# A fused two-layer block on one core: the first stage in another order, and feature chunks read contiguously

## The chip, the cores and the metric

The kernel runs on one core of one Trainium2 chip. The metric is the device time in microseconds; runs of the kernel before took 401.86, 402.31 and 403.27 us, median 402.31. One program computes everything: PE (matrix products), DVE and ACT (vector and scalar work), POOL, and SP, which issues the transfers, each follow a list of instructions of their own and wait for each other through counting semaphores.

## The reference

Six blocks are added one after the other to x, which is 2 sequences of 64 tokens with 512 features, so 128 rows:

```python
x = x + _L0_xattn_ref(_layernorm(x), ctx_512, Wq, w_kc_q, w_kc_kv, W_qr, W_kr, Wo)
x = x + _L0_attn_ref(_layernorm(x), wq, wk, wv, wo)        # weights replaced by sign(w) * mean|w|
x = x + _L0_ffn_ref(_layernorm(x), gate_w, w_gate, w_up, w_down)   # 32 experts, top 8
x = x + _L1_xattn_ref(_layernorm(x), ctx_512, Wq, Wkv_expand, Wout)
x = x + _L1_attn_ref(_layernorm(x), w_qkv, w_g, w_proj, gn_weight, gn_bias)
x = x + _L1_ffn_ref(_layernorm(x), w_router, w_gate, w_up, w_down, ...)
```

Most of the change is in the first block, an attention over a context of 1024 tokens with 16 heads:

```python
q_big = einsum('bshk,hkq->bshq', (hidden_q @ Wq.T).reshape(b, s, H, K), w_kc_q)
kv_rope = kv_c * cos + rotate_half(kv_c) * sin
q_r = einsum('bshq,hqr->bhsr', q_big, W_qr)
k_r = einsum('bld,hdr->bhlr', kv_rope, W_kr)
attn = softmax(einsum('bhsr,bhlr->bhsl', q_r, k_r))
ctx_c = einsum('bhsl,bld->bhsd', attn, kv_rope)
out = einsum('bhsd,hkd->bshk', ctx_c, w_kc_kv).reshape(b, s, H * K) @ Wo.T
```

## The kernel before

All data are 32-bit floats. The weights of the first block come in four groups of four heads. For each group g, PE does five things, and the program names them so:

- `queries(g)` (L988): the query projection, 16 products of 128 columns, from `in_wq` (1024 KB) and the transposed x, `xnT`.
- `qrk_products(g)` (L978): w_kc_q times W_qr of the four heads, from `in_wr` (1152 KB, the rank weights), 12 products whose outputs are 64 partitions high: even heads go to PSUM partitions 0 to 63, odd heads to 64 to 127 (column halves).
- `qkw_products(g)` (L1012): that times W_kr (`in_wkr`, 512 KB), 4 products over 64 rows. These are the key products.
- `latent_queries(g)` (L1022): that times the queries, 4 products. Its result, `qk_x`, is the query in the space of the context.
- `context_transposes(g)` (L1001): a quarter of the rotated context, 4 transposes.

An instruction of this kind on 32-bit data appears twice in the trace (16 products are x32). Between them DVE copies from PSUM: `at_copy` (L631) after qrk, `bw_copy` (L637) after qkw, `qk_copy` (L643) after latent; ACT copies the queries (L426) and the context (L422). The rotation of the context is shared by POOL (L385, the swapped half times sine, into `rope_tmp`) and DVE (L621, times cosine; L624, the addition). SP issues all transfers on one queue in a fixed order. `keep_clock(n)` (L957) is n products that nobody reads, which keep PE busy while it has nothing to do.

Then come 16 units of one head pair and one sequence (the unit loop): two products of scores (L1056), DVE's row maximum (L666), ACT's exponential (L439), eight transposes (L1066), copied half by ACT (L447) and half by DVE (L673), eight context products (L1075), a reciprocal (L677) and a scaling on DVE (L681), one transpose (L1084) and its copy (L452). They are pipelined: in step i PE does the scores of unit i, the transpose of result i-3, the context products of unit i-2 and the transposes of unit i-1. The next block's weights (`we`, from `in_e`) lie in SBUF by then; for them DVE sums absolute values (L696, in steps 8 to 11: 2048, 512, 512 and 2048 columns), and ACT takes all signs at once (L472, 5120 columns, in step 12).

Wherever x is transposed (L965, six times; L1214, twice; L1387, once) and in the gather of rows for the experts (L1263), the 512 features are split into four chunks with feature 4q+c in chunk c, so that a chunk is every fourth number of a row; the weights are laid out to match.

## Time and profile before

| what | value |
|---|---|
| profiled execution | 405.05 us, of which the span is 403.0 us |
| PE | busy 382.4 us, 95% of the span |
| DVE, ACT, POOL | 38%, 21%, 6% of the span |
| transfers | 79.41 MB, 197 GB/s mean; first part of the program about 300 to 450 GB/s |
| DVE in a unit (L666, L673, L677, L681) | 1.22, 0.69, 0.15 and 0.35 us |
| ACT in a unit (L439, its read-out, L447, L452) | 1.12, 0.19, 0.59 and 0.28 us |
| gather (L1263) on the chain of waits | groups of four at 0.91 or 0.92 us (ten) and 1.04 us (two), one of eight at 1.98 us |
| output projection of the retention (L1391) | 8 instructions, 5.41 us from 348.49; granted clock 0.50 from 350 to 352 us |

The span is the time from the first to the last instruction; what lies around it belongs to the execution too. The chain of waits is read backwards by the profiler, from the last instruction to what released it. A row of the timeline gives the start, the duration, the engine, the line, and in brackets how long the engine stood idle before it and who released it. The granted clock is a share of 2.4 GHz.

### The profile page before, as it was taken

How to read it: one execution, taken by the hardware profiler on the slowest of the kernel's cores; microseconds unless marked ns; L12 is line 12 of the kernel's file. 1: busy time of each engine (PE TensorE's matmuls, PEld its weight loads, DVE VectorE, ACT ScalarE, POOL GpSimd, SP SyncE). 2: the span in 40 equal slices, each digit the busy share in tenths (PEclk: the TensorE clock that was granted, in tenths of full speed). 3: DMA queues.
4: the chain of work that ended last, by engine and by line, in shares of the span. 5: the costliest groups of instructions: out<-in, count | busy, mean ns of one | idle time of the engine just before them, and what ended most of it. 6: DMA issues, size and time to landing. Idle time of an engine off the chain costs nothing.

```text
span 403.0 us, 5245 instructions
## 1 busy us (share of the span) xinstructions
PE 382.4 (95%) x2175; PEld 240.8 (60%) x2175; DVE 151.3 (38%) x326; ACT 85.0 (21%) x163; POOL 23.5 (6%) x45
## 2 busy tenths in 40 slices
PE   9898899999889999999999999999989999899997
PEld 7787668777678575666444544444356546564456
DVE  3164254576632145235022222222265344544221
ACT  1001144434742004102121212212102024101011
POOL 1050000000000010011000000000020100000220
PEclk9899999999999999999999999999999999899999
DMA  8999699800003200060798889989689600000000
GB/s 306 362 422 445 228 426 433 344 2 0 2 0 110 126 2 0 2 260 2 262 386 313 340 337 325 371 298 443 260 337 423 285 0 2 0 2 0 0 0 26
DMA packets 7591, 79.41 MB, mean 197 GB/s; under 512 B 977, under 2 KB 1745, under 8 KB 2513
## 3 DMA queue, kind: packets, MB, share of 16 engines
q1 hardware_dynamic: 7568, 79.09, 49.8%
q8 instruction: 17, 0.28, 0.3%
q14 instruction: 6, 0.04, 0.0%
HBM read 78.82 MB, written 0.26 MB: 196 GB/s over the span
## 4 chain that ended last, share of the span: by engine, by line
PE 80%; DVE 10%; issue 3%; DMA 3%; POOL 2%; ACT 1%; SPq 0%; ACTq 0%; DVEq 0%; POOLq 0%
PE ps L1276 9%; PE ps L1404 9%; PE ps L1075 6%; PE ps L1056 4%; PE ps L1303 4%; PE ps L1301 4%; PE ps L1348 3%; PE ps L1114 3%; PE ps L1263 3%; PE ps L988 3%; PE ps L1308 3%; PE ps L1066 3%; PE ps L1236 3%; DMA rd<-in_wkr 3%; PE ps L1219 2%
## 5 line engine op out<-in xcount | busy, mean ns | idle before, releaser
L957 PE MATMUL ps<-ones 128*128 128x256 bf16 x305 | 38.7, 279 | 1.0 <-POOL ones L368 1.0
L1276 PE MATMUL ps<-rd,ra 128*64 128x384 f32 x224 | 39.2, 492 | 0.0
L957 PEld LDWEIGHTS ps<-ones 128*128 128x128 bf16 x305 | 30.1, 100 | 8.3 <-issue 3.2
L1075 PE MATMUL ps<-rd,ra 128*128 128x128 f32 x256 | 31.4, 276 | 0.0
L1075 PEld LDWEIGHTS ps<-rd,ra 128*128 128x128 f32 x256 | 29.9, 192 | 2.3 <-issue 2.0
L1056 PE MATMUL ps<-rd 128*128 128x512 f32 x64 | 30.0, 594 | 0.7 <-DVE rd L643 0.7
L1276 PEld LDWEIGHTS ps<-rd,ra 128*64 128x64 f32 x224 | 14.8, 136 | 25.6 <-issue 25.6
L1404 PE MATMUL ps<-rd,xnT 128*128 128x512 f32 x64 | 28.0, 594 | 0.0
L439 ACT ACTIVATE ra<-ps,sv 128x1024 f32<-128x1024 f32 x16 | 17.8, 1115 | 37.9 <-DVE sv L666 37.9
L831 DVE COPY xnT<-ps 128x512 f32<-128x512 f32 x14 | 9.7, 691 | 39.5 <-PE ps L1303 39.5
L666 DVE TENSOR_REDUCE sv<-ps 128x1 f32<-128x1024 f32 x16 | 19.6, 1223 | 8.5 <-PE ps L1056 8.5
L673 DVE COPY ra<-ps 128x512 f32<-128x512 f32 x16 | 11.1, 692 | 25.1 <-PE ps L1066 25.0
L1404 PEld LDWEIGHTS ps<-rd,xnT 128*128 128x128 f32 x64 | 11.9, 190 | 14.2 <-issue 14.2
L817 DVE SCALAR_TENSOR_TENSOR ra<-ra,ps 128x192 f32<-128x192 f32 x14 | 5.0, 354 | 40.9 <-ACT ra L516 40.9
L516 ACT ACTIVATE ra<-ps 128x192 f32<-128x192 f32 x14 | 4.6, 331 | 61.0 <-PE ps L1276 61.0
L1066 PE MATMUL ps<-cst,ra 128*128 128x128 f32 x128 | 16.6, 273 | 0.8 <-ACT ra L439 0.8
L1263 PEld LDWEIGHTS ps<-ra,xn 128*128 128x128 f32 x56 | 14.8, 321 | 3.6 <-issue 2.4
L988 PE MATMUL ps<-xnT,ra 128*128 128x128 f32 x128 | 16.9, 295 | 0.0
L988 PEld LDWEIGHTS ps<-xnT,ra 128*128 128x128 f32 x128 | 16.2, 209 | 0.4
L1056 PEld LDWEIGHTS ps<-rd 128*128 128x128 f32 x64 | 11.0, 190 | 9.1 <-issue 8.1
L1308 PE MATMUL ps<-xnT,ra 128*128 128x512 f32 x28 | 14.5, 601 | 1.4 <-DVE xnT L831 1.4
L1303 PE MATMUL ps<-rd,ra 128*128 128x512 f32 x28 | 15.8, 645 | 0.0
(231 smaller groups left out, 501.9 us busy)
## 6 DMA issues: line engine op xcount, KB each, us to landing
rd<-in_ring SPq DMA_DIRECT2D x16, 2304.0 KB, 9.0
rd<-in_f1gu SPq DMA_DIRECT2D x8, 1024.0 KB, 13.2
rb<-in_wb SPq DMA_DIRECT2D x1, 5120.0 KB, 35.5
ra<-in_e SPq DMA_DIRECT2D x2, 2560.0 KB, 9.4
rb<-in_b SPq DMA_DIRECT2D x1, 5120.0 KB, 20.2
ra<-in_wr SPq DMA_DIRECT2D x4, 1152.0 KB, 16.5
ra<-in_wq SPq DMA_DIRECT2D x4, 1024.0 KB, 20.4
ra<-in_f1s SPq DMA_DIRECT2D x1, 2048.0 KB, 29.3
```

Source lines behind the costliest of these rows:

```text
L439: act.activation(prob_x[u % 2].rearrange("p j l -> p (j l)"), ps[:, 2 * (u % 2):2 * (u % 2) + 2, :].rearrange("p a n -> p (a n)"), ACT.Exp ...
L666: dve.tensor_reduce(mx_x[:, u:u + 1], ps[:, 2 * (u % 2):2 * (u % 2) + 2, :].rearrange("p a n -> p (a n)"), AX.X, ALU.max, negate=True).the ...
L957: pe.matmul(ps[:, bank, 0:256], idle[:, 0:P], idle, start=True, stop=True)
L988: ins = pe.matmul(ps[:, g % 2, h * P:(h + 1) * P], wq_x(g)[:, c, h * P:(h + 1) * P], xnT[:, c, :], start=(c == 0), stop=(c == C - 1))
L1056: ins = pe.matmul(ps[:, 2 * (u % 2) + half, :], rows, kvT[:, u % 2, half * 512:half * 512 + 512], start=True, stop=True)
L1066: ins = pe.transpose(ps[:, 4 + half, j * P:(j + 1) * P], prob_x[u % 2][:, 4 * half + j, :], ident)
L1075: ins = pe.matmul(ps[:, 6, 0:P], probT_x[u % 2][:, j, :], kvr[:, u % 2, j, :], start=(j == 0), stop=(j == J - 1))
L1263: ins = pe.matmul(ps[:, half, c * 256:(c + 1) * 256], src[:, 2 * half + c, :], placed[:, 4 * q:4 * q + 4, :].rearrange("p e s -> p (e s)") ...
L1276: ins = pe.matmul(ps[CAP * e:CAP * e + CAP, 2 + p % 2, 0:2 * I0].rearrange("p (g n) -> p g n", g=2), moe_xq[q % 2][:, c, CAP * e4:CAP * e4 ...
L1303: pe.matmul(ps[:, 4, :], hT[:, 1, :], slot_down[j][:, 2, :], start=False, stop=True).then_inc(dn_done, 1)
L1308: return pe.matmul(ps[:, 7, :], moe_hT_even[(p - DENSE) // 2 % 2][:, 2 + p % 2, :], moe_y, start=False, stop=last)
L1404: ins = pe.matmul(ps[:, bank, 0:n], xnT[:, c, :], w[:, c, lo:lo + n], start=(c == 0), stop=(c == C - 1))
```

## The change

The transfers of the first stage begin with x, the constants, the query weights and then the rank weights of each group. `in_wkr` is laid out on 128 partitions with half the columns, even heads on 0 to 63 and odd heads on 64 to 127. PE's list begins with the transposes of x and the queries, and the last key product and the last latent product stand between the first scores.

On PE, from the start of the program to the second pair of scores, the instructions of before are these (the first line is `keep_clock`):

```order
L957 MATMUL ps<-ones 128x256 x44
L978 MATMUL ps<-ra 64x128 x12
L965 MATMUL ps<-cst,xn 128x128 x4
L957 MATMUL ps<-ones 128x256 x16
L1012 MATMUL ps<-rd 128x128 x4
L988 MATMUL ps<-xnT,ra 128x128 x16
L978 MATMUL ps<-ra 64x128 x12
L1022 MATMUL ps<-rd 128x128 x4
L1012 MATMUL ps<-rd 128x128 x4
L988 MATMUL ps<-xnT,ra 128x128 x16
L978 MATMUL ps<-ra 64x128 x12
L1022 MATMUL ps<-rd 128x128 x4
```

and now, where L962 are the transposes of x, L987 the queries, L975 qrk, L1013 the key products and L1023 latent:

```order
L954 MATMUL ps<-ones 128x256 x40
L962 MATMUL ps<-cst,xn 128x128 x4
L954 MATMUL ps<-ones 128x256 x16
L987 MATMUL ps<-xnT,ra 128x128 x16
L975 MATMUL ps<-ra 64x128 x12
L987 MATMUL ps<-xnT,ra 128x128 x16
L1013 MATMUL ps<-rd 128x128 x4
L975 MATMUL ps<-ra 64x128 x12
L1023 MATMUL ps<-rd 128x128 x4
L987 MATMUL ps<-xnT,ra 128x128 x16
L1013 MATMUL ps<-rd 128x128 x4
L1000 MATMUL ps<-cst,rd 128x128 x4
```

The first two groups of queries have moved ahead of the first key products, and the third stands before any context transpose.

On PE at the end of the stage, before (L1047 transposes `ctx64`, L1056 are the scores, L1066 the transposes of the first unit):

```order
L988 MATMUL ps<-xnT,ra 128x128 x16
L1001 MATMUL ps<-cst,rd 128x128 x4
L1022 MATMUL ps<-rd 128x128 x4
L1047 MATMUL ps<-cst,ctx 128x128
L1056 MATMUL ps<-rd 128x512 x4
L1066 MATMUL ps<-cst,ra 128x128 x8
```

and now (L1037 are the scores, L1049 the transposes of the first unit):

```order
L1000 MATMUL ps<-cst,rd 128x128 x4
L1023 MATMUL ps<-rd 128x128 x4
L1037 MATMUL ps<-rd 128x512 x2
L1013 MATMUL ps<-rd 128x128 x4
L1037 MATMUL ps<-rd 128x512 x2
L1023 MATMUL ps<-rd 128x128 x4
L1110 MATMUL ps<-cst,ctx 128x128
L1049 MATMUL ps<-cst,ra 128x128 x8
```

A key product and a latent product now stand between the scores and the transposes that need the first exponential.

On DVE in a unit with a sum of absolute values, before (L666 row maximum, L673 copy, L677 and L681 reciprocal and scaling, L696 the sum):

```order
L666 TENSOR_REDUCE sv<-ps 128x1
L673 COPY ra<-ps 128x512
L677 RECIPROCAL sv<-sv 128x1
L681 TENSOR_SCALAR xn<-ps,sv 128x128
L696 TENSOR_REDUCE sv<-ra 128x1
```

and now (L659, L670, L674, L666, L693 in the same sense):

```order
L659 TENSOR_REDUCE sv<-ps 128x1
L670 RECIPROCAL sv<-sv 128x1
L674 TENSOR_SCALAR xn<-ps,sv 128x128
L666 COPY ra<-ps 128x512
L693 TENSOR_REDUCE att_st<-ra 128x1
```

The scaling has moved ahead of the copy; the sum is one of six, of at most 1024 columns.

The diff, cut to its core:

```diff
-        rope_tmp = rd[:, 4096:5120].rearrange("p (j d) -> p j d", j=J)
+        rope_tmp = [rd[:, 3072 + 1024 * b:4096 + 1024 * b].rearrange("p (j d) -> p j d", j=J) for b in range(B)]
+        we_parts = [(0, 0, 1024), (1, 2048, 2560), (2, 2560, 3072), (3, 3072, 4096), (0, 1024, 2048), (3, 4096, 5120)]
...
             sp.dma_start(x[:, :], x_in).then_inc(ld_x, 16)
-            rank_weights(0)
             sp.dma_start(cst[:, :], consts_d).then_inc(ld_const, 16)
             query_weights(0)
-            sp.dma_start(rd[0:R0, 11264:13312], wkr_d).then_inc(ld_kr, 16)
+            rank_weights(0)
+            sp.dma_start(rd[:, 11264:12288], wkr_d).then_inc(ld_kr, 16)
+            query_weights(1)
             rank_weights(1)
             sp.dma_start(rd[:, 0:2048], ctx_d).then_inc(ld_ctx, 16)
             sp.dma_start(rd[:, 2048:3072], rope_d).then_inc(ld_ctx, 16)
-            for g in range(1, GROUPS):
-                if g > 1:
-                    rank_weights(g)
+            for g in range(2, GROUPS):
                 query_weights(g)
+                rank_weights(g)
...
+            sp.wait_ge(q_ps, 3)
+            sp.wait_ge(at_ps, 3)
+            sp.dma_start(we, e0_d).then_inc(ld_e0, 16)
             sp.wait_ge(qk_ps, GROUPS)
-            sp.dma_start(we, e0_d).then_inc(ld_e0, 16)
...
-                if i == 12:
-                    act.wait_ge(asum_done, 4)
-                    act.activation(we, we, ACT.Sign).then_inc(sign_done, 1)
+                if 6 <= i < 12:
+                    _, a0, a1 = we_parts[i - 6]
+                    act.wait_ge(asum_done, i - 5)
+                    act.activation(we[:, a0:a1], we[:, a0:a1], ACT.Sign).then_inc(sign_done, 1)
...
-                src = xn[:, :].rearrange("p (q c) -> p c q", c=C)
+                src = xn[:, :].rearrange("p (c q) -> p c q", c=C)
...
-                for h in range(4):
-                    ins = pe.matmul(ps[:, 4 + g % 2, h * P:(h + 1) * P], qrk[0:R0, 4 * g + h, :], wkrT[0:R0, 4 * g + h, :],
-                                    start=True, stop=True)
+                for j in range(2):
+                    for odd in range(2):
+                        rows = slice(odd * R0, odd * R0 + R0)
+                        ins = pe.matmul(ps[:, 4 + odd, j * P:(j + 1) * P], qrk[rows, 2 * g + j, :], wkrT[rows, 2 * g + j, :],
+                                        start=True, stop=True)
...
             def scores(u):
-                if u == 0:
-                    pe.wait_ge(qk_sb, GROUPS)
+                pe.wait_ge(qk_sb, u // 4 + 1)
+                if u < 2:
+                    pe.wait_ge(kvT_sb, 2 * u + 2)
+                    pe.wait_ge(q_sb, GROUPS)
+                    pe.wait_ge(at_sb, GROUPS)
```

POOL no longer waits for DVE between the two halves of the rotation, DVE copies qrk in one piece instead of two, and `bw_copy` reads both PSUM banks of the row halves at once; each key product now waits for the copy of the one before. The same contiguous split stands in the transposes of L1214, L1387 and L1448 and in the gather, and every weight that meets such a chunk is laid out by rows of 128 on the host, with rows as long as before.

## Rows read from the trace of the kernel before

**Rows 1.** Chain of waits, 0 to 54 us: start us, us, what

```profile
2.57 10.43 DMA rd<-in_wkr
...
14.26 5.39 PE ps L988 x32
19.66 1.46 PE ps L978 x24
21.12 1.09 PE ps L1022 x8
...
26.49 3.20 POOL rd L385 x2
...
29.78 1.23 DVE rd L624
...
32.99 3.77 PE ps L988 x32
```

**Rows 2.** Timeline of PE, 0 to 54 us: start us, us, then idle before

```profile
0.98 6.42 PE L957 MATMUL ps<-ones 128*128 128x256 bf16 x44 [0.98 <-POOL ones L368]
...
9.38 1.91 PE L957 MATMUL ps<-ones 128*128 128x256 bf16 x16
13.14 1.13 PE L1012 MATMUL ps<-rd 64*128 64x128 f32 x8 [1.85 <-DMA rd<-in_wkr]
...
31.83 1.16 PE L1012 MATMUL ps<-rd 64*128 64x128 f32 x8 [1.79 <-DVE rd L631]
...
45.72 1.13 PE L1022 MATMUL ps<-rd 128*128 128x128 f32 x8 [0.30 <-issue]
...
47.70 3.70 PE L1056 MATMUL ps<-rd 128*128 128x512 f32 x8 [0.74 <-DVE rd L643]
52.23 1.09 PE L1066 MATMUL ps<-cst,ra 128*128 128x128 f32 x8 [0.84 <-ACT ra L439]
```

**Rows 3.** Windows: busy us, then PEclk, DMA share, GB/s

```profile
14.00:16.00 2.00, 2.00 (x11) 1.88 (x10) 0.69 (x1) 0.00 (x0) 0.00 (x0) 0.55 1.02 424
...
8.00:14.00 6.00, 4.15 (x44) 3.56 (x40) 1.53 (x3) 0.00 (x0) 0.00 (x0) 1.00 1.01 295
14.00:34.00 20.00, 18.21 (x160) 16.91 (x159) 9.89 (x15) 1.79 (x3) 5.46 (x4) 0.91 1.05 434
```

**Rows 4.** Chain of waits, 60 to 128 us: the scores of three units

```profile
75.65 1.72 PE ps L1056 x4
...
80.14 1.72 PE ps L1056 x4
...
114.37 1.72 PE ps L1056 x4
```

**Rows 5.** Timeline of SP's queue: issue of the third rank weights

```profile
5.26 0.45 SPq L289 DMA_DIRECT2D ra<-in_wr  x1
```

**Rows 6.** DMA issues of the window 5.2 to 5.5 us: us to landing last

```profile
DMA to landing us min/median/max: 20.5/20.5/20.5
```

**Rows 7.** Timeline, 80 to 121 us, of DVE, ACT and PE

```profile
85.73 2.28 DVE L696 TENSOR_REDUCE sv<-ra 128x1 f32<-128x2048 f32 x1
...
104.97 4.48 ACT L472 ACTIVATE ra<-ra 128x5120 f32<-128x5120 f32 x1
...
120.09 0.33 PE L1084 MATMUL ps<-cst,xn 128*128 128x128 f32 x1 [1.24 <-DVE xn L681]
```

**Rows 8.** Weight loads by form, 200 to 210 us: busy us, mean ns

```profile
L1263 PEld LDWEIGHTS ps<-ra,xn 128*128 128x128 f32 x7 | 1.9, 321 | 0.4 <-issue 0.2
...
L1308 PEld LDWEIGHTS ps<-xnT,ra 128*128 128x128 f32 x2 | 0.3, 191 | 0.0
```

**Rows 9.** Chain of waits, 145 us to the end

```profile
145.99 0.76 PE ps L965 x4
...
308.00 0.66 PE ps L1191 x4
...
394.99 1.73 PE ps L1425 x8
```

More of the change, by code:

```diff
@@ L623, in rope @@
                 dve.wait_ge(rope_swap, b + 1)
-                dve.tensor_tensor(kvr[:, b], kvr[:, b], rope_tmp, ALU.add).then_inc(rope_ready, 1)
+                dve.tensor_tensor(kvr[:, b], kvr[:, b], rope_tmp[b], ALU.add).then_inc(rope_ready, 1)
             def at_copy(g):
                 dve.wait_ge(at_ps, g + 1)
-                heads = qrk[0:R0, 4 * g:4 * g + 4, :].rearrange("p (j two) k -> p two j k", two=2)
-                for odd in range(2):
-                    ins = dve.tensor_copy(heads[:, odd], ps[odd * R0:odd * R0 + R0, 2 + g % 2, 0:2 * P].rearrange(
-                        "p (j k) -> p j k", j=2))
-                ins.then_inc(at_sb, 1)
+                dve.tensor_copy(qrk[:, 2 * g:2 * g + 2, :].rearrange("p j k -> p (j k)"),
+                                ps[:, 2 + g % 2, 0:2 * P]).then_inc(at_sb, 1)
             def bw_copy(g):
                 dve.wait_ge(bw_ps, g + 1)
-                dve.tensor_copy(qkw[:, 4 * g:4 * g + 4, :].rearrange("p h t -> p (h t)"), ps[:, 4 + g % 2, :]).then_inc(bw_sb, 1)
+                dve.tensor_copy(qkw[:, 4 * g:4 * g + 4, :].rearrange("p (j two) d -> p two j d", two=2),
+                                ps[:, 4:6, 0:2 * P].rearrange("p two (j d) -> p two j d", j=2)).then_inc(bw_sb, 1)
             def qk_copy(g):
@@ L654, in _ @@
             rope(1)
-            for g in range(2, GROUPS):
-                at_copy(g)
-                qk_copy(g - 1)
-                bw_copy(g)
-            qk_copy(GROUPS - 1)
-            dve.wait_ge(c64T_ps, 1)
-            dve.tensor_copy(ctx64T[:, :], ps[:, 7, 0:P]).then_inc(c64T_ready, 1)
+            bw_copy(1)
+            at_copy(2)
+            qk_copy(1)
+            bw_copy(2)
+            at_copy(3)
+            qk_copy(2)
             def row_max(u):
@@ L983, in queries @@
                 pe.wait_ge(ld_q[g], 16)
+                if g == 0:
+                    pe.wait_ge(xT_ready, 1)
                 if g >= 2:
@@ L1092, in latent_values @@
                 ins.then_inc(lat_ps, 1)
+            pe.wait_ge(consts_ready, 1)
+            keep_clock(40)
+            pe.wait_ge(ld_const, 16)
+            x_transposes(0)
+            queries(0)
+            qrk_products(0)
+            queries(1)
+            qkw_products(0)
+            qrk_products(1)
+            latent_queries(0)
+            queries(2)
+            qkw_products(1)
+            context_transposes(0)
+            qrk_products(2)
+            context_transposes(1)
+            latent_queries(1)
+            queries(3)
+            context_transposes(2)
+            qkw_products(2)
+            qrk_products(3)
+            context_transposes(3)
+            latent_queries(2)
             for i in range(UNITS + 3):
@@ L1096, in _ @@
                     scores(i)
+                if i == 0:
+                    qkw_products(GROUPS - 1)
+                if i == 1:
+                    latent_queries(GROUPS - 1)
+                    pe.wait_ge(kvT_sb, GROUPS)
+                    pe.wait_ge(ld_c64, 16)
+                    pe.transpose(ps[:, 7, 0:P], ctx64[:, :], ident).then_inc(c64T_ps, 1)
                 if i == UNITS + 1:
@@ L1119, in _ @@
             latent_values(3)
-            pe.wait_ge(asum_done, 4)
+            pe.wait_ge(asum_done, 6)
             pe.wait_ge(consts_ready, 2)
-            pe.matmul(ps[:, 5, 0:4], ones[:, :], asum, start=True, stop=True).then_inc(wsum_ps, 1)
+            for half in range(2):
+                ins = pe.matmul(ps[:, 5, 0:4], ones[:, :], asum[:, half], start=(half == 0), stop=(half == 1))
+            ins.then_inc(wsum_ps, 1)
             output_product(range(8, 12))
@@ L1510 @@
     cst, rope, xpos, decay = constants()
-    wq = v["L0_xattn_Wq"].T.reshape(P, C, GROUPS, 512)
+    rows = lambda w: w.reshape(-1, P, w.shape[1]).transpose(1, 0, 2).reshape(P, -1)
+    wq = rows(v["L0_xattn_Wq"].T).reshape(P, C, GROUPS, 512)
     wkcq = v["L0_xattn_w_kc_q"].transpose(2, 0, 1).reshape(P, KQ, H0, P)
@@ L1522 @@
     q0 = v["L0_attn_wq"].T.reshape(D, 8, 4, 16).transpose(0, 2, 1, 3).reshape(D, D)
[L1523 to L1525 removed]
+    e0 = np.concatenate([rows(q0), rows(v["L0_attn_wk"].T), rows(v["L0_attn_wv"].T), rows(v["L0_attn_wo"].T)], axis=1)
+    pair = lambda w: w.reshape(PAIRS, 2, C, P, I0).transpose(0, 3, 1, 2, 4).reshape(PAIRS, P, -1)
     wd = v["L0_ffn_w_down"].reshape(PAIRS, 2, I0, D)
```

111 lines of the change are left out of this document (44 added, 67 removed).

## The prediction

> **What bounds the kernel now.** I read the busy time first: PE is busy for 95% of the span (the table), so only work taken off PE, PE's own gaps and PE's clock can be worth anything. DVE and ACT count only where PE stands behind them. Then I read the chain of waits of the first 54 us. After one transfer (wkr, 10.43 us from issue to landing) it is PE nearly throughout, but for one stretch in which POOL and DVE rotate the context [rows 1]. PE's timeline shows its gaps there: 1.85 us for wkr, 1.79 us for a DVE copy queued behind the rotation, then 0.30, 0.74 and 0.84 us where the first score unit waits for the last copies and the first exponential [rows 2]. That is 5.5 us. After the first gap the granted clock is 0.55 of full from 14 to 16 us, so mostly the lower level, 1.2 GHz [rows 3], and the 32 query products of the first group take 5.39 us on the chain, against 3.77 us for a later group at full clock [rows 1]. In the unit loop the scores stand 4.49 us apart while nothing disturbs them (75.65 and 80.14), and PE has no gap: PE bounds it. But from 80.14 to 114.37 seven units take 34.23 us, not 31.43: 2.8 us lost [rows 4].
>
> **First stage.** By its new order PE runs 40 idle products, the transposes, queries(0), qrk(0), queries(1), qkw(0), qrk(1), latent(0), queries(2), and so on. Only one product sits where the new wait falls, so I walk there. The idle products take 6.42/44 = 0.146 us each from 0.98 us on [rows 2], so 40 end at 6.8 us, 0.6 us before the 7.4 of now. x and the constants are the first two transfers, and queries(0)'s weights make 1510 KB in all. Now x, the first rank weights and the constants are 1638 KB and have landed when the transposes run, ahead of the 16 idle products of 9.38 [rows 2]; so queries(0) has its data when the new 16 (1.91 us) end, at 6.8 + 0.6 + 1.9 = 9.3 us. Then, at full-clock durations, query 3.77, qrk 1.46, query 3.77, qkw 0.85 (below), qrk 1.46, latent 1.09 [rows 1]: PE stands before queries(2) at 21.7 us.
>
> When do its weights land? Before them lie 256+230+1024+1152+512+1024+1152+1024+512 KB, with them 7910 KB. Now the rank weights of group 2 complete 8038 KB and land at 5.26+20.5 = 25.8 us [rows 5, 6]; at 434 GB/s 128 KB less are there 0.3 us sooner, at 25.5 us. But wkr now fills 128 partitions instead of 64. From 8 to 14 us, when it goes through, the queues move 295 GB/s at a DMA share of 1.01, against 434 GB/s from 14 to 34 us at 1.05 [rows 3]. At 434 the 1.77 MB of those 6 us would take 4.1 us: 1.9 us earlier. So 23.6 us, and PE waits 1.9 us (bounds: 0 if copies delay PE by as much, 3.8 if the port gain fails). Beside it, the Trainium skill, page "SBUF — State Buffer", section "Door 1: The DMA port swizzle", says that partitions 0 to 63 reach 8 of 16 ports. By its about 218 GB/s against 436 for 512 KB this would be an estimate of 1.2 us; the trace's drop is wider, and I keep its 1.9.
>
> A wait of 1.85 us was followed by the low clock, one of 1.79 us (from 30.04) was not. A wait of 1.9 us before queries(2) is nearest to the first, so I count the fall once more: 5.39-3.77 = 1.6 us lost.
>
> The rotation: POOL's two buffers let it run both batches without waiting for DVE. Now its second swap takes 3.20 us in the chain, then 1.23 us of DVE [rows 1], then copies, then PE. With context and tables landed at about 21 us, two swaps of at most 3.2 us and a 1.23 us addition end by 28.7 us. PE needs the first batch after queries(2) and qkw(1), at 23.6+5.4+0.85 = 29.9 us. So the rotation hides, with 1 us to spare; the copy queued behind it (0.69 us) is wanted by latent(1), another 2.4 us on. The last key product and latent(3) move beside the first scores, so that 1.16+1.13 us of PE work stands where PE waited 0.74 and 0.84 us [rows 2]; DVE takes their copies after the first row maxima, while scores(1) (1.7 us) runs. I take all these gaps (5.5 us) as gone, cost zero.
>
> Key products in row halves: four pieces of 1.16 us [rows 2], each 4 products on 64 rows. The trace has no row pair. Its nearest row is column halves (L978): 24 instructions in 1.46 us against 8 in 1.09 us for whole ones (L1022) [rows 1], 0.061 against 0.136 us each, so halves do run together. But those loads are 64 columns wide and these are 128, and a load is nearly as long as its product. Bounds: no gain, or 0.55 of the time, 0.5 us saved a piece; a loss of 0.1 us a piece if switching costs what one issue gap does. I take the middle, 0.25 us, 1.0 us in all, since the slow load is the nearer likeness.
>
> The Trainium skill, page "TensorEngine Tiling (Array Packing)", section "Key Properties", says that changing the tiling mode drains TensorE. By that the pieces would gain less. The rows show qrk (column halves) from 19.66 for 1.46 us and whole products from 21.12 [rows 1], without a pause between them; for row halves no row here shows it, and a drain of 0.1 us at each of eight changes would make the time 0.8 us longer.
>
> Sum of the stage: 5.5 + 1.6 + 0.6 + 1.0 - 1.9 - 1.6 = 5.2 us gained at the third pair of scores (now 53.32).
>
> **Sums and signs in pieces.** DVE's reduction over 2048 columns takes 2.28 us and delays the next row maximum; ACT's sign over 5120 takes 4.48 us and the exponential behind it starts late; PE then waits [rows 7]. The pieces are at most 1024 wide: by the same rates 1.2 and 0.9 us. In a free unit DVE works 1.22+0.69+0.15+0.35 = 2.4 us and ACT 1.12+0.19+0.59+0.28 = 2.2 us of 4.49 (the table), and a piece fits in what is left. So the 2.8 us go. e0 is issued earlier, behind wb; it lands well before the sixth unit. Also the scaling of the context now stands ahead of the copy of the transposed probabilities. At the loop's end PE waits 1.24 us for that scaling (L681), which DVE does after copy and reciprocal [rows 7]. In the new order it is done during the transposes, and the context product then waits only for the copy (0.69 us): 0.5 us. Loop: 3.3 us. One more tiny product for the sums: nothing I can tell.
>
> **Contiguous chunks.** The gather's weight loads read every fourth number: 321 ns, against 191 ns for L1308's contiguous ones [rows 8]. Four gather products take 0.91 to 1.04 us on the chain (the table), where 8 of the same width with contiguous loads take 1.73 us [rows 9], 0.87 us for four. Over 56 of them (one group of 8 at 1.98, two of 4 at 1.04, ten at 0.91) it is 13.2 against 12.1 us: 1.1 us. The transposes of xn take 0.76 us for four, those of contiguous data 0.66 us [rows 9]; nine such groups stand alone on the chain: 0.9 us. Together 2.0 us (bounds 0 and 2.3).
>
> The same page on SBUF, section "Door 1", says that fp32 may stride by 4 for free. By that this part would bring nothing. The loads' 321 against 191 ns [rows 8] speak against it, so it is a rival with a small chance.
>
> **Sum.** 5.2 + 3.3 + 2.0 = 10.5 us. The profiled execution took 405.05 us for its span of 403.0; it would take 394.6. It lies 2.7 us over the median of the runs, 402.31, and I take the same difference off that: 391.8 us.
>
> **Rivals.**
> - The clock holds after the wait for queries(2), as after 1.79 us now: 391.8 - 1.6 = 390.2 us. For it: the two gaps differ by 0.06 us only. Chance 0.24.
> - The row halves run fully together (1.0 us more) and the clock holds: 389.2 us. For it: column halves do. Against: width of the loads. Chance 0.10. With these goes the stretch at 348 us, where the clock is at 0.50 after two short gaps and eight projection products cost 5.41 us for some 3.4 (the table). It may fall otherwise when all lies 10 us earlier: 2.0 us to the good.
> - The transfers land as late as now: queries(2) waits 3.8 us: 393.7 us. Against: 295 GB/s only while wkr passes. Chance 0.13.
> - Strided loads are hidden behind their products: no 2.0 us: 393.8 us. Chance 0.06.
> - The pieces still hold up the loop, since sums and signs now touch six units: the 2.8 us stay, 394.6 us. Against: DVE's 2.4 us of 4.49. Chance 0.05.
> - Slower than before: PE waits for each of the query weights in turn and the clock stays at its low level from the first query product on. Low clock costs (5.39-3.77)/3.77 = 0.43 of the work; the stage has 33 us of it: 14.2 us more, less the 1.6 counted: 391.8 + 12.6 = 404.4 us. It decides from about 28 us of full-clock work done at the low level ((10.5 + 1.6)/0.43). Against: now the next group at 19.66 runs at its full-clock 1.46 us [rows 1] once work flows, and I see only one wait. Chance 0.02.
> The forecast itself has 0.40.
>
> **Numbers.** Forecast 391.8 us. Range 388.4 to 394.6 us: it holds the forecast, the clock, port and load cases, and leaves out some 0.1 at each side. A difference of 0.3% (1.2 us) is what a measurement of this kernel can tell from none. Faster by more: 0.96; within: 0.02; slower: 0.02.
>
> **What would show it.** In the changed profile: PE without a gap until about 21.7 us, then one gap of about 2 us before queries(2) on in_wq, and the clock low in the next stretch; no gap at the context transposes; key products of 0.9 us a group; third scores near 48 us; scores 4.49 us apart to the end of the loop; the gather's loads near 190 ns and 0.87 us for four. I am wrong if a wait for a copy replaces the gaps, if the 0.5 clock spreads over several query products, or if loads stay at 320 ns.

## The result, and the profile after

The changed kernel takes 391.86 us (median of 4 runs, 390.99 to 393.28); on the same chip the kernel before took 402.79 us (4 runs). The ratio is 0.9713, with a 95% interval of 0.9668 to 0.9758. The forecast of 391.8 us was met. Its terms were not all right, though: three of them were off by 0.8 to 1.8 us each, and the errors cancelled by luck.

Line numbers have shifted: queries L987, qrk L975, key products L1013, latent L1023, context transposes L1000, scores L1037, transposes of the first unit L1049, residual projection L1128, gather L1279, output projection of the retention L1407, `keep_clock` L954.

PE's timeline after, start of the program to the scores, answers to [rows 2]:

```profile
0.98 5.90 PE L954 MATMUL ps<-ones 128*128 128x256 bf16 x40 [0.98 <-POOL ones L371]
...
9.55 3.84 PE L987 MATMUL ps<-xnT,ra 128*128 128x128 f32 x32 [0.48 <-DMA ra<-in_wq]
13.32 1.53 PE L975 MATMUL ps<-ra 128*64 128x128 f32 x24
16.05 3.84 PE L987 MATMUL ps<-xnT,ra 128*128 128x128 f32 x32 [1.21 <-DMA ra<-in_wq]
19.82 0.71 PE L1013 MATMUL ps<-rd 64*128 64x128 f32 x8
20.46 1.53 PE L975 MATMUL ps<-ra 128*64 128x128 f32 x24
21.93 1.16 PE L1023 MATMUL ps<-rd 128*128 128x128 f32 x8
25.08 3.84 PE L987 MATMUL ps<-xnT,ra 128*128 128x128 f32 x32 [1.99 <-DMA ra<-in_wq]
28.84 0.71 PE L1013 MATMUL ps<-rd 64*128 64x128 f32 x8
29.49 0.66 PE L1000 MATMUL ps<-cst,rd 128*128 128x128 f32 x4
```

The old gaps (for wkr, for the copy behind the rotation, and the three small ones at the first scores) are gone. In their place PE waits three times, 3.68 us in all, and each time for query weights. After its first product, which waits 0.98 us for POOL as before, it waits nowhere in the first 47 us for DVE, ACT or POOL.

The windows of [rows 3] after (busy us of PE, PEld, DVE, ACT, POOL, then PEclk, DMA share, GB/s):

```profile
8.00:14.00 6.00, 5.52 (x54) 5.04 (x54) 0.52 (x3) 0.58 (x1) 0.00 (x0) 1.00 1.01 421
14.00:16.00 2.00, 0.85 (x16) 0.60 (x12) 0.42 (x1) 0.02 (x1) 0.00 (x0) 1.00 1.02 420
14.00:34.00 20.00, 16.80 (x177) 15.25 (x174) 11.43 (x13) 2.41 (x5) 6.46 (x4) 1.00 1.05 437
```

The transfers run at 421 GB/s where they ran at 295, and the granted clock is 1.00 in all three windows, although PE stood still for 1.99 us. So every query group takes 3.74 or 3.84 us, the first too. Before, it took 5.39 us on the chain [rows 1], and in the same view as above:

```profile
14.19 5.46 PE L988 MATMUL ps<-xnT,ra 128*128 128x128 f32 x32
```

The chain of waits after, at the scores and in the first part of the loop:

```profile
42.56 0.65 PE ps L1013 x8
...
46.99 1.72 PE ps L1037 x4
...
100.74 1.72 PE ps L1037 x4
105.23 1.73 PE ps L1037 x4
```

The third scores start at 46.99 instead of 53.32 us: the stage is 6.3 us shorter. From there to the last scores at 105.23 us thirteen units take 58.24 us, 4.48 each, without the 2.8 us that were lost in [rows 4]; the first product of the residual projection starts at 117.97 in the timeline of PE, where it was 127.61. Of this 9.6 us the stage holds 6.3 and the loop 3.3.

The end of the loop on PE, and DVE in a unit with a sum, which answer to [rows 7]:

```profile
110.25 0.30 PE L1069 MATMUL ps<-cst,xn 128*128 128x128 f32 x1 [0.53 <-ACT ra L451]
```

```profile
82.82 0.69 DVE L666 COPY ra<-ps 128x512 f32<-128x512 f32 x1 [0.47 <-PE ps L1049]
83.43 1.21 DVE L693 TENSOR_REDUCE att_st<-ra 128x1 f32<-128x1024 f32 x1
84.56 1.21 DVE L659 TENSOR_REDUCE sv<-ps 128x1 f32<-128x1024 f32 x1
```

The wait of 1.24 us for the scaling has become 0.53 us for a copy of ACT, and the row maximum follows at once on the sum.

Behind the loop, in the chain of waits, the first gather group and the projection of the retention:

```profile
178.32 1.73 PE ps L1279 x8
...
337.32 3.71 PE ps L1407 x8
```

and the weight loads of the gather, 195 to 205 us (busy us, mean ns), which answer to [rows 8]:

```profile
L1279 PEld LDWEIGHTS ps<-ra,xn 128*128 128x128 f32 x4 | 0.8, 190 | 0.5 <-issue 0.5
```

The loads take 190 ns where they took 321. The group of eight went from 1.98 to 1.73 us, the groups of four to 0.86 or 0.87, and four transposes from 0.76 to 0.67. Over 13 gather groups and the eight groups of transposes behind the loop that is 1.8 to 1.9 us. Another 1.7 us comes from L1407, 3.71 against 5.41 us, and the change has no part in that: before, the granted clock was 0.50 from 350 to 352 us, and after it is 1.00 there. PE's waits just ahead of these products are the same in both (0.79 and 0.78 us before, 0.79 twice after).

The profiled execution took 391.82 us, 13.2 us less than that of before, but the medians are only 10.9 us apart. The profile of before had its clock at the lower level in two places, which cost 3.3 us in all (1.6 and 1.7), and an execution of before does not always have them (below).

### The profile page after: what moved, and what is told of

It reads as the page before. It is cut to its first block, busy times and chain, and to the rows that moved or that the text cites. A ratio compares the mean times of both kernels' runs of the same rounds, so it can differ in the third digit from the quotient of the medians.

```text
span 390.0 us, 5266 instructions
## 1 busy us (share of the span) xinstructions
PE 374.0 (96%) x2173; PEld 231.6 (59%) x2173; DVE 151.9 (39%) x324; ACT 85.4 (22%) x168; POOL 24.6 (6%) x46
## 4 chain that ended last, share of the span: by engine, by line
PE 83%; DVE 8%; DMA 5%; SPq 1%; POOL 1%; issue 1%; ACT 0%; POOLq 0%; DVEq 0%
PE ps L1292 10%; PE ps L1420 9%; PE ps L1037 7%; PE ps L1060 7%; DMA ra<-in_wq 5%; PE ps L1319 4%; PE ps L1317 4%; PE ps L1364 4%; PE ps L1128 4%; PE ps L1049 3%; PE ps L1324 3%; PE ps L1279 3%; PE ps L1252 3%; PE ps L1235 2%; PE ps L1173 2%; PE ps L987 2%
## 5 line engine op out<-in xcount | busy, mean ns | idle before, releaser
L954 PE MATMUL ps<-ones 128*128 128x256 bf16 x301 | 38.2, 279 | 1.0 <-POOL ones L371 1.0
L954 PEld LDWEIGHTS ps<-ones 128*128 128x128 bf16 x301 | 29.6, 100 | 8.1 <-issue 3.2
L1037 PE MATMUL ps<-rd 128*128 128x512 f32 x64 | 30.2, 594 | 0.0
L659 DVE TENSOR_REDUCE sv<-ps 128x1 f32<-128x1024 f32 x16 | 19.6, 1223 | 10.7 <-PE ps L1037 10.7
L987 PE MATMUL ps<-xnT,ra 128*128 128x128 f32 x128 | 15.3, 277 | 3.7 <-DMA ra<-in_wq 3.7
L987 PEld LDWEIGHTS ps<-xnT,ra 128*128 128x128 f32 x128 | 14.6, 192 | 4.4 <-DMA ra<-in_wq 4.4
L1049 PE MATMUL ps<-cst,ra 128*128 128x128 f32 x128 | 16.6, 273 | 0.0
L1037 PEld LDWEIGHTS ps<-rd 128*128 128x128 f32 x64 | 10.9, 190 | 7.8 <-issue 7.6
L1317 PE MATMUL ps<-rd,ra 128*64 128x512 f32 x56 | 15.1, 618 | 0.0
L1364 PE MATMUL ps<-rb,xnT 128*128 128x512 f32 x32 | 14.3, 595 | 0.2 <-DVE xnT L599 0.2
## 6 DMA issues: line engine op xcount, KB each, us to landing
rd<-in_f1gu SPq DMA_DIRECT2D x8, 1024.0 KB, 13.2
ra<-in_f1s SPq DMA_DIRECT2D x1, 2048.0 KB, 25.8
```

The source lines that it names most:

```text
L659: dve.tensor_reduce(mx_x[:, u:u + 1], ps[:, 2 * (u % 2):2 * (u % 2) + 2, :].rearrange("p a n -> p (a n)"), AX.X, ALU.max, negate=True).the ...
L954: pe.matmul(ps[:, bank, 0:256], idle[:, 0:P], idle, start=True, stop=True)
L987: ins = pe.matmul(ps[:, g % 2, h * P:(h + 1) * P], wq_x(g)[:, c, h * P:(h + 1) * P], xnT[:, c, :], start=(c == 0), stop=(c == C - 1))
L1037: ins = pe.matmul(ps[:, 2 * (u % 2) + half, :], rows, kvT[:, u % 2, half * 512:half * 512 + 512], start=True, stop=True)
L1049: ins = pe.transpose(ps[:, 4 + half, j * P:(j + 1) * P], prob_x[u % 2][:, 4 * half + j, :], ident)
L1317: pe.matmul(ps[CAP * e:CAP * e + CAP, 4, :], hT[:, 0, CAP * e:CAP * e + CAP], slot_down[j][:, e, :], start=True, stop=False)
```

## Experiments

**1. Only the contiguous chunks (c_only).** The kernel before with the new layout of the features, the weights laid out to match, and nothing else:

```diff
-                src = xn[:, :].rearrange("p (q c) -> p c q", c=C)
+                src = xn[:, :].rearrange("p (c q) -> p c q", c=C)
...
```

> The kernel before with the contiguous feature chunks alone. My theory: gather products from 13.2 to about 12.1 us on the chain of waits and nine groups of four transposes from 0.76 to 0.67 us, 1.9 us in all, so about 400.6 us where the kernel before takes 402.5. Rival (the loads are hidden behind their products): within 0.5 us of the kernel before. What the profile shows at the projection after 346 us (5.41 us before, 3.71 us after the change) should not depend on this edit but on the clock: 5.4 or 3.7 us, with a granted clock that goes with it.

Measured: 401.12 us (nine runs from 399.75 to 402.93 and one of 405.86) against 402.47, ratio 0.9964, interval 0.9938 to 0.9989. In its chain of waits:

```profile
186.48 1.73 PE ps L1263 x8
194.00 0.87 PE ps L1263 x4
...
345.47 3.71 PE ps L1391 x8
```

The gather and the transposes have the durations of the changed kernel, so the part stands alone and is worth 1.8 us in the trace; the medians show 1.4 us, within the interval. L1391 takes 3.71 us here too, in the old order of the first stage: its 5.41 us belonged to one execution and not to the kernel.

**2. Only the loop (l_only).** The kernel before with the sums and signs in six pieces and the scaling ahead of the copy:

```diff
-                if 1 <= i <= UNITS:
-                    probT_copy(i - 1)
                 if i >= 2:
                     ctx_scale(i - 2)
+                if 1 <= i <= UNITS:
+                    probT_copy(i - 1)
...
+                if 9 <= i < 15:
+                    _, a0, a1 = we_parts[i - 9]
+                    act.wait_ge(asum_done, i - 8)
+                    act.activation(we[:, a0:a1], we[:, a0:a1], ACT.Sign).then_inc(sign_done, 1)
...
```

> The kernel before with the sums and signs in six pieces of at most 1024 columns (in the units 8 to 13 for the sums, 9 to 14 for the signs) and the scaling ahead of the copy. My theory: scores stand 4.49 us apart from 53 us to the end of the loop, and the loop is 3.3 us shorter: about 399.2 us against 402.5. Rival (the pieces only spread the stall over more units): units of more than 4.6 us, and less than 1 us gained.

Measured: 399.5 us (398.15 to 401.73, 8 runs), ratio 0.9927, interval 0.9887 to 0.9967: 3.0 us by the medians. Three of its scores in the chain of waits:

```profile
60.50 1.72 PE ps L1056 x4
...
105.39 1.72 PE ps L1056 x4
109.87 1.73 PE ps L1056 x4
```

Eleven units take 49.37 us, 4.49 each. The loop's term holds by itself.

**3. The old order in DVE's unit (old_scale).** The changed kernel with the copy of the transposed probabilities ahead of the scaling again (the first two hunks of the diff above, backwards).

> The changed kernel with DVE's old order in a unit: the copy of the transposed probabilities ahead of the scaling of the context. By my sum the new order is worth 0.5 us, all at the end of the loop: PE waits about 1.2 us for the scaling there again, in place of a shorter wait for the copy, and the time is near 392.3 us. Rival, the new order is worth nothing there because the copy is as late: the same stretch from the last scores to the context product keeps its length, and the time stays at 391.9 us.

Measured: 393.36 us (392.91 to 393.82, 4 runs), ratio 0.9753, interval 0.9688 to 0.9818. In its timeline the old wait of [rows 7] is back, to the hundredth:

```profile
111.60 0.33 PE L1069 MATMUL ps<-cst,xn 128*128 128x128 f32 x1 [1.24 <-DVE xn L674]
```

From the third scores (47.64 us on its chain) to the first product of L1128 (119.12) it takes 71.48 us, against 70.98 in the changed kernel: the 0.5 us predicted. The medians differ by 1.5 us. Of the rest, 0.65 us is the later start of the third scores in its profile; three of its four executions have a mean clock of 0.996, which is not this order's doing either. The first stage is that of the changed kernel, and here PE waits much longer before queries(2), without a fall of the clock behind it:

```profile
25.63 3.84 PE L987 MATMUL ps<-xnT,ra 128*128 128x128 f32 x32 [3.15 <-DMA ra<-in_wq]
```

**4. Halves in turn, or one kind after the other (same_half).** A first theory was that the key products gain because neighbours in the list lie on different rows. Here the two even ones come first:

```diff
-                for j in range(2):
-                    for odd in range(2):
+                for odd in range(2):
+                    for j in range(2):
```

> The changed kernel with its four key products of a group in another order: both of the upper half, then both of the lower, instead of in turn. Theory (products on different row halves run together): a group of 8 instructions takes about 1.0 us instead of 0.65, because only the middle two differ in their half; the first stage is up to 1.0 us longer (three of the four groups are past the last wait for weights). Rival (the 0.65 us come from something else, as the copy layout or the banks): 0.65 us as now, no difference.

Measured: 391.34 us (390.38 to 391.69, 4 runs), ratio 0.9722, interval 0.9699 to 0.9744.

```profile
19.44 0.72 PE L1013 MATMUL ps<-rd 64*128 64x128 f32 x8
```

The group takes 0.72 us against 0.71 in the changed kernel: this theory falls. The order inside a group of four makes no difference.

**5. All four on the same rows (one_half).** The banks, the order and the layout of the transfer stay those of the changed kernel; only the products of odd heads are computed from the even heads' rows.

```diff
-                        rows = slice(odd * R0, odd * R0 + R0)
+                        rows = slice(0, R0)
```

> The changed kernel with all four key products of a group read from partitions 0 to 63, into the same two PSUM banks and in the same order; so the products of the odd heads are those of the even heads' numbers, and the output is not the reference's. Row halves as the cause: nothing can run side by side any more, and a group of key products takes about 1.1 us in the timeline of PE as before, with its eight weight loads near 0.96 us, instead of 0.71 and 0.52; four groups make it 1.6 to 1.8 us slower than the changed kernel, near 393.4 us. Rival, the two banks or the smaller transfer layout as the cause: a group stays at 0.71 us and the time at 391.9 us.

Measured: 392.81 us (391.88 to 394.3, 4 runs), ratio 0.9728, interval 0.9663 to 0.9793. Its timeline of PE, and its loads from 18 to 22 us:

```profile
21.11 1.16 PE L1013 MATMUL ps<-rd 64*128 64x128 f32 x8
```

```profile
L1013 PEld LDWEIGHTS ps<-rd 64*128 64x128 f32 x8 | 1.0, 187 | 0.1
```

and the same view of the changed kernel:

```profile
L1013 PEld LDWEIGHTS ps<-rd 64*128 64x128 f32 x8 | 0.5, 186 | 0.1
```

The group is back at 1.16 us. The two PSUM banks and the wide transfer bring nothing to it: it is the row halves. One load still lasts 187 ns, but eight are busy for 1.0 us in one case and for 0.5 in the other, so the loads lie over each other more when their halves differ. The time shows less of it than the 1.6 to 1.8 us expected, 1.0 us between the medians: from queries(2) to the third scores it takes 23.1 us on the chain (26.39 to 49.47) against 21.9, which holds three of the four groups, and the first group lies ahead of a wait. Whether two halves could also write into one bank was not tried.

**6. W_kr in two transfers of 64 partitions (kr_two).** Same bytes, same places, but each transfer fills one half of the partitions:

```diff
-            sp.dma_start(rd[:, 11264:12288], wkr_d).then_inc(ld_kr, 16)
+            sp.dma_start(rd[0:R0, 11264:12288], wkr_d[0:R0]).then_inc(ld_kr, 16)
+            sp.dma_start(rd[R0:P, 11264:12288], wkr_d[R0:P]).then_inc(ld_kr, 16)
...
-                    pe.wait_ge(ld_kr, 16)
+                    pe.wait_ge(ld_kr, 2 * 16)
```

> The changed kernel with the 512 KB of W_kr moved as two transfers of 64 partitions each instead of one of 128. Theory (a transfer to 64 partitions moves at about half the rate): 256+256 KB at about 210 GB/s, some 1.2 us later for everything behind; waits for query weights grow by about that, from 1.21 to 2.4 us before queries(1) and with no further growth before queries(2), and the time is 1.2 us longer (393.0), or 2.8 longer if the clock falls after the longer wait. Rival (the transfers overlap, since the two halves use different ports, or the slowness had another reason): 421 GB/s from 8 to 14 us as now, no difference.

Measured: 395.01 us (394.01 to 396.43, 4 runs), ratio 0.9811, interval 0.9786 to 0.9835: 3.2 us of the gain gone, more than either number expected. Timeline of PE, then windows:

```profile
20.20 6.60 PE L988 MATMUL ps<-xnT,ra 128*128 128x128 f32 x32 [4.74 <-DMA ra<-in_wq]
```

```profile
8.00:14.00 6.00, 5.55 (x52) 5.19 (x51) 1.16 (x3) 0.48 (x1) 0.00 (x0) 1.00 1.02 273
...
20.00:26.00 6.00, 5.80 (x27) 5.80 (x28) 0.00 (x0) 0.00 (x0) 0.00 (x0) 0.50 1.02 423
```

The rate from 8 to 14 us falls to 273 GB/s, below the 295 of [rows 3], and the weights of queries(1) land 4.1 us later, at 20.2 us instead of 16.0. PE waits 4.74 us, and the clock goes to 0.50 behind it: that group takes 6.60 us. So the 128 partitions are what made the transfers faster. The one rival left by this run alone, two transfers instead of one, falls with the kernel before, which had a single transfer of 64 partitions: its order of transfers shows 295, 324, 303 and 329 GB/s from 8 to 14 us in four profiles, against 415 to 427 in the nine profiles in which W_kr goes to 128 partitions at once. The Trainium skill, page "SBUF — State Buffer", section "Door 1: The DMA port swizzle", says that 64 partitions reach half of the ports; the direction agrees with this trace. By the section's about 218 GB/s for 64 partitions against 436 for 128, 512 KB would lose 1.2 us, an estimate; the trace shows 4.1 us at the transfer behind (2.9 us against the latest of the other profiles with the changed kernel's order of transfers, 17.3 us in experiment 5): the measurement decides.

**7. The weights of queries(2) ahead of the context (wq2_early).** If the wait of 1.99 us is the loss, it should go when these weights come sooner:

```diff
+            query_weights(2)
             sp.dma_start(rd[:, 0:2048], ctx_d).then_inc(ld_ctx, 16)
             sp.dma_start(rd[:, 2048:3072], rope_d).then_inc(ld_ctx, 16)
-            for g in range(2, GROUPS):
-                query_weights(g)
-                rank_weights(g)
+            rank_weights(2)
+            query_weights(3)
+            rank_weights(3)
```

> The changed kernel with the third query weights ahead of the context and the rope tables. Theory (PE waits 1.99 us because the 1536 KB of context and tables lie ahead): the weights are there 3.7 us sooner and this wait is gone, but the tables land at about 25 us instead of 22.6, POOL and DVE rotate until some 34 us, and PE waits for the first context transposes instead, at about 27 us, for 1 to 3 us: the time changes by -1 to +1 us. Rival (the rotation has slack): 2 us shorter, 389.9 us.

Measured: 395.16 us (394.34 to 395.89, 4 runs), ratio 0.9818, interval 0.979 to 0.9846: 3.3 us slower than the changed kernel, where -1 to +1 us was expected.

```profile
22.80 3.74 PE L988 MATMUL ps<-xnT,ra 128*128 128x128 f32 x32
26.46 0.71 PE L1014 MATMUL ps<-rd 64*128 64x128 f32 x8
30.63 1.09 PE L1001 MATMUL ps<-cst,rd 128*128 128x128 f32 x4 [3.45 <-DVE rd L621]
31.65 2.63 PE L976 MATMUL ps<-ra 128*64 128x128 f32 x24
```

The wait is gone and a longer one stands in its place: the rotation now starts later (POOL at 24.98 us instead of 22.63), and PE stands 3.45 us before the context transposes, after which the clock is low (24 products of qrk in 2.63 us instead of 1.53). The old wait hid the rotation. I had given it 1 us to spare in my prediction; moving one 1 MB transfer was enough to lose that cover.

**8. Idle products in the waits (fill).** Ten before queries(1) and 16 before queries(2):

```diff
+            keep_clock(10)
             queries(1)
...
+            keep_clock(16, 7)
             queries(2)
```

> The changed kernel with 10 idle products in the wait before queries(1) and 16 in the one before queries(2), which fit in the waits. Theory (the clock held in these waits in all runs): no difference, 391.9 us. Rival (the clock falls in some runs, which makes the spread from 390.99 to 393.28 us): the runs lie within 1 us of each other near 391 us.

Measured: 392.53 us (391.98 to 393.05, 4 runs), ratio 0.975, interval 0.9722 to 0.9779. queries(2) starts at 25.26 us, as without them (25.08): the idle products end at 25.19, and on the chain of waits the weights land at 25.21, so the transfer still sets this point. Four executions, one of them at a mean clock of 0.996, don't tell whether the filling keeps the clock up more often.

**9. The kernel before once more (before2).** No edit.

> The kernel before once more, for the granted clock of each of its executions. If the half clock at 14 and at 348 us (1.6 and 1.7 us) belongs to the kernel, every execution shows a mean clock near 0.992 and times near 402.5; if it is chance, executions without one or the other lie 1.6 to 3.3 us lower and show up to 1.000.

Measured: 402.69 us (401.66 to 405.71, 10 runs). In its profiled execution (402.68 us) the low clock stands at another place than in [rows 2]:

```profile
13.99 3.84 PE L988 MATMUL ps<-xnT,ra 128*128 128x128 f32 x32
...
22.77 5.46 PE L988 MATMUL ps<-xnT,ra 128*128 128x128 f32 x32 [1.31 <-DMA ra<-in_wq]
```

The first query group has the full clock here, and one group later it falls, after a wait of 1.31 us. Of 58 timed executions of this kernel on four chips whose mean clock is known, 19 have 0.999 or 1.00 and took 401.5 to 402.5 us, 20 have 0.996 (402.3 to 403.8), 14 have 0.992 (404.0 to 405.7) and 5 have 0.987 (406.2 to 408.9). The profile with one fall has a mean of 0.996 and the one with two 0.992, so each fall seems to take 0.004 off it, and 0.987 would be three, which no profile here shows. A fall is something that an execution has or has not, and the profiled 405.05 us was one with two.

The first waits differ as well. In place of 1.85 us for wkr and 1.79 us behind the rotation [rows 2], this profile has 0.40 us and none, and the 1.31 us before queries(1) instead. Experiments 1 and 2, which keep this first stage, have 0.87 and 1.04 us, then 1.62 and 1.40 us before queries(1), then 0.74 us behind the rotation in both, and their clock held. The last three waits (0.30, 0.74 and 0.84 us) are the same in all four profiles.

**10. The changed kernel once more (after_again).** No edit.

> The changed kernel itself once more, beside the version with the queries first on the same chip. Executions at full clock should lie at 391 to 393 us. If the start of the stage is a matter of how the transfers come in an execution, the wait before queries(2) varies by some tenths of a microsecond to 1.5 us from the 1.99 us of the first profile, and with it the third pair of scores (46.99 us).

Measured: 393.04 us (390.41 to 394.65, 6 runs) against 404.13 (11 runs), ratio 0.9731, interval 0.9686 to 0.9776.

```profile
15.72 3.84 PE L987 MATMUL ps<-xnT,ra 128*128 128x128 f32 x32 [1.06 <-DMA ra<-in_wq]
...
24.78 5.46 PE L987 MATMUL ps<-xnT,ra 128*128 128x128 f32 x32 [2.03 <-DMA ra<-in_wq]
```

Here is the fall that the prediction counted: a wait of 2.03 us before queries(2), then 5.46 us for the group, 1.6 us more than 3.84. Four of these six executions have a mean clock of 0.995 or 0.996, and none of the first four had. After 1.99 us the clock held, after 2.03 it fell. Three more profiles with this order of the first stage held it as well: after 2.00 us (experiment 4), 1.57 us with 2.15 us one group earlier (experiment 5), and 3.15 us (experiment 3). The length of the wait alone doesn't decide it in this range.

**11. and 12. Queries first (fast1, fast_again).** From experiments 6 to 8: keep the bandwidth, let PE have more to do before it needs later weights, and keep something ahead of the rotation. The query weights of groups 1 and 2 come ahead of the rank weights, and PE's list follows:

```diff
             query_weights(0)
+            query_weights(1)
             rank_weights(0)
             sp.dma_start(rd[:, 11264:12288], wkr_d).then_inc(ld_kr, 16)
-            query_weights(1)
+            query_weights(2)
             rank_weights(1)
...
             queries(0)
-            qrk_products(0)
             queries(1)
+            qrk_products(0)
+            queries(2)
             qkw_products(0)
             qrk_products(1)
             latent_queries(0)
-            queries(2)
             qkw_products(1)
+            keep_clock(4, 7)
+            latent_queries(1)
+            queries(3)
...
```

The context transposes follow behind queries(3), and ACT's and DVE's copies stand in the new order.

> The changed kernel with both transfers and PE's list led by queries: weights of queries 0 and 1 first, then rank 0, W_kr, queries 2, rank 1, context and tables, queries 3, rank 2 and 3; PE does queries(0), queries(1), qrk(0), queries(2), and so on. By 413 KB a us from 9.5 us on, every transfer but the fourth query weights lands before PE wants it: the waits for query weights fall from 3.7 to about 1 us, and the kernel is 2.5 us shorter (389.4 us) if the rotation stays hidden. Rival (the rotation by POOL and DVE, which is 6.5 us long when both work, becomes the bound): a wait at the context transposes or at the latent products eats 1 us or more of it.

Measured: 390.16 us (388.94 to 391.33, 4 runs), ratio 0.9685, interval 0.9648 to 0.9721.

```profile
9.60 7.41 PE L987 MATMUL ps<-xnT,ra 128*128 128x128 f32 x64
16.95 1.53 PE L975 MATMUL ps<-ra 128*64 128x128 f32 x24
18.99 3.84 PE L987 MATMUL ps<-xnT,ra 128*128 128x128 f32 x32 [0.51 <-DMA ra<-in_wq]
...
35.42 0.71 PE L1013 MATMUL ps<-rd 64*128 64x128 f32 x8 [0.74 <-DVE rd L625]
...
45.52 1.02 PE L1037 MATMUL ps<-rd 128*128 128x512 f32 x2
```

The waits are 0.51, 0.26 and 0.74 us, the last two of them for DVE, as the rival had it, and the third scores start at 45.52 in this view (46.83 in the changed kernel's). Once more beside the changed kernel, on one chip:

> The version with the queries first, in which the query weights of groups 1 and 2 come ahead of the rank weights, once more. By its first profile it has 1.5 us of waits in the stage instead of 3.7 and should be 1.5 us faster than the changed kernel on the same chip, so near 390.3 us. Rival: the difference between the two was one of chips, and both have the same time within 0.5 us.

Measured: 389.81 us (389.52 to 391.83, 6 runs), ratio 0.9662, interval 0.9624 to 0.97, where the changed kernel on the same chip had 393.04. All ten executions of this version have a mean clock of 1.00. It beats both kernels: by 3.2 us over the changed one on this chip (1.7 us between the medians of their first runs), part from the shorter waits and part because no execution of it shows a fall. How much of it remains at the same clock rests on few executions: the two of the changed kernel on this chip with 1.00 took 390.41 and 392.11 us.

## Why the prediction came out, step by step

The third scores were to start at 48.1 us and start at 46.99. The point between is queries(2): predicted for 23.6 us, it starts at 25.08, 1.5 us late; from there to the third scores I had 24.5 us and it takes 21.9, which is 2.6 us less.

- **The gaps, 5.5 us: right for the profile it was read from.** All five are gone, and no copy took their place. The first two were not constants of the kernel (experiment 9). The rotation is hidden, as walked through, though the copy behind it has nothing to spare (last section).
- **The first query group, 1.6 us, and the fewer idle products, 0.6 us.** Right: the group has its 3.84 us, and 40 idle products took 5.90 us. That queries(0) then waits 0.48 us for its weights, which takes back most of the 0.52 us that the idle products saved, belongs to the next term: I had taken from [rows 2] that these bytes are there.
- **The new wait, 1.9 us: mis-sized in total and right by accident where I put it.** The wait before queries(2) is 1.99 us. But PE comes there 1.4 us later than I said (23.1 and not 21.7), above all because of a wait of 1.21 us before queries(1) that I did not look for: I walked only to the place where I expected the trouble. And the weights land at 25.03 us and not at 23.6 (24.7 to 26.4 us in the five other profiles with this order of transfers). In all 3.68 us of waiting instead of 1.9, nearly what the rival "as late as now" gave (3.8), though not by its mechanism, a port gain that fails. The port gain itself is real: 421 instead of 295 GB/s from 8 to 14 us is 0.76 MB more, 1.8 us, as I had it. What I left out is around it. In the first 8 us the queues move less than before (349 and 368 GB/s from 4 to 6 and 6 to 8 us, where before had 394 and 444), which gives back 0.3 MB or 0.7 us; and another 0.7 us goes to later transfers that run ahead at the same time: when the weights of queries(2) are complete, 9.3 MB have moved, though only 8.1 MB stand before them and in them (before: 9.1 MB and 8.2 MB at 25.8 us).
- **The clock falls again, 1.6 us: right as a chance, wrong as a term.** It did not fall in the first profile and did in the second (experiment 10), at just this place and for just this price: once in the five profiles with this order of the first stage and a wait before queries(2). I had weighed 1.85 against 1.79 us of waiting as if their order decided it. The second profile of the kernel before (1.31 us, fell), the pair 1.99 and 2.03, and 3.15 us without a fall (experiment 3) show that it doesn't.
- **Row halves, 1.0 us: mis-sized.** A group takes 0.65 us on the chain instead of 1.10, so 1.8 us for four, of which three groups, 1.3 us, lie behind the last wait for weights; the upper bound was the better likeness (experiment 5). The loads of 128 columns, which I held against it, lie over each other as well. The Trainium skill, page "TensorEngine Tiling (Array Packing)", section "Key Properties", speaks of a drain when the tiling mode changes; in this trace key products at 19.82 for 0.71 us are followed by qrk at 20.46 without a gap, so no drain can be seen beside the gain.
- Of the 2.6 us, 1.6 is the clock and 0.6 the three key products that lie behind queries(2); 0.4 us no run isolates. The chain has candidates that more than cover it: the last two latent products take 0.89 us each instead of 1.09 and 1.14, and the transposes of the first unit 0.87 instead of 1.09.
- **Sums, signs and scaling, 3.3 us: right** (3.3 in the profile, 3.0 alone in experiment 2; the 0.5 us for the scaling in experiment 3). The extra product for the sums, which I put at nothing, costs 0.2 us: the tiny products of L1137 take 0.51 us in the timeline after, those of L1122 before 0.28.
- **Contiguous chunks, 2.0 us: right**, 1.8 us in the trace. The rival by the Trainium skill, page "SBUF — State Buffer", section "Door 1: The DMA port swizzle" (fp32 may stride by 4 for free), falls for weight loads: the loads take 321 against 190 ns, and experiment 1 has the gain in isolation.
- **From the profile to the median.** I took the 2.7 us between the profiled 405.05 and the median off as it stood. It was not a constant of the kernel but about two falls of the clock. Compared at full clock, executions of before take about 401.9 us and the first four of after 391.9: 10.0 us. The terms without any clock give the same: 6.3 - 1.6 for the stage, 3.3 for the loop, 1.8 for the chunks, 9.8 in all. My 10.5 held 1.6 us of clock gained and 1.6 lost again, so its clock terms cancelled, and it is 0.7 us too much: the waits 1.8 more than counted and the chunks 0.2 less, against 0.8 for the row halves and half a microsecond that no run isolates.

So the total was met within 0.1 us by errors that cancelled, which was luck. The parts that each have an experiment of their own (loop, chunks, scaling) were right to 0.2 or 0.3 us; the three that were off all concern the start, where transfers, clock and PE act on each other.

## What to carry to other kernels

When transfers are put in another order, write down the landing time of every one that the bounding engine needs and walk through all of them: a wait that an earlier one causes moves the later ones, and a long wait may be the cover of work on another engine that shows when it goes. A stretch of low clock in one profile is one draw: read the mean clock of many executions before a term is made of it, and compare kernels at the same clock. Products of 64 rows are worth pairing over both row halves (a group of four went from 1.10 to 0.65 us), and numbers that are loaded as weights are worth laying side by side (321 to 190 ns a load).

## What the runs showed of the hardware

- The start is a draw too. The same 40 idle products took 5.90 us in the first profile of the changed kernel and 6.47 in the second, and between 6.47 and 7.32 in the profiles of experiments 3 to 8, 11 and 12.
- After a wait of 1.31, 1.85, 2.03, 3.45 or 4.74 us the granted clock fell, at a price of 1.5 to 2.8 us; after 1.40, 1.57, 1.62, 1.79, 1.99, 2.00, 2.15 and 3.15 us it did not. At 348 us it fell in one profile of the kernel before after two waits of 0.79 and 0.78 us, for 1.7 us.
- DVE and POOL slow each other. In the changed kernel POOL's four pieces of the rotation run without a pause; the first two take 1.15 us each and the last two 2.14. Three of DVE's four pieces beside them take nearly twice their old 1.22 us; the fourth runs after POOL has ended. In the kernel before, one pair overlaps (DVE at 26.33, POOL at 26.49), and there DVE keeps its 1.22 us and POOL's piece takes 2.08. POOL, then DVE:

```profile
22.63 6.46 POOL L387 TENSOR_TENSOR rd<-rd 128x512 f32<-128x512 f32 x4 [17.06 <-DMA rd<-in_rope]
```

```profile
23.79 2.18 DVE L617 TENSOR_TENSOR rd<-rd 128x1024 f32<-128x1024 f32 x1
26.00 2.06 DVE L620 TENSOR_TENSOR rd<-rd 128x1024 f32<-128x1024 f32 x1
27.99 2.17 DVE L617 TENSOR_TENSOR rd<-rd 128x1024 f32<-128x1024 f32 x1
30.20 1.23 DVE L620 TENSOR_TENSOR rd<-rd 128x1024 f32<-128x1024 f32 x1
```

So the rotation ends at 31.4 us and not by 28.7 as I had it. It hides all the same: its first batch, which PE needs at 29.49, is ready at 28.1. The copy queued behind it on DVE (L630) starts at 31.34 and takes 0.68 us, and latent(1), which needs it, starts at 32.08: there is nothing to spare at that place.
- A transfer of 512 KB in two halves of 64 partitions delays the 1 MB transfer behind it by 4.1 us, and the loss does not end with the narrow transfer: from 14 to 20 us the queues still move 351 GB/s there, against 422.
